# A first attention's scores in 64-row halves, with maxima in single banks

## The reference

```python
scores = jnp.einsum('bhqd,bhkd->bhqk', q, k) / SCALING
att = jax.nn.softmax(scores, axis=-1)
out = jnp.einsum('bhal,bhlv->bhav', att, v)
```

## Time and profile before

| | us |
|---|---|
| median of 3 runs | 1371.28 (1370.59 to 1373.99) |
| profiled execution, its span | 1372.0 |
| TensorE busy in it | 1249.1 |
| VectorE busy | 1009.4 |
| ScalarE busy | 851.8 |
| GpSimd busy | 237.5 |
| line 725, score products, 1024 of them | 312.4 |
| line 612, reductions, 507 of them | 595.8 |
| line 670, exponentials, 1024 of them | 555.6 |

### The profile page before, as it was taken

The page is one execution under the profiler, slowest core; times in us unless marked ns, Lnnn a source line. Parts: engine busy times, 40 slices in busy tenths (PEclk is TensorE's granted clock), DMA queues, the critical chain, the costliest instruction groups (busy, mean ns, idle before and its releaser), DMA issues. The chain is left out here.

```text
span 1372.0 us, 25967 instructions
## 1 busy us (share of the span) xinstructions
PE 1249.1 (91%) x10305; PEld 580.1 (42%) x10305; DVE 1009.4 (74%) x1288; ACT 851.8 (62%) x1447; POOL 237.5 (17%) x309
## 2 busy tenths in 40 slices
PE   6968999999999999999999978998899899899980
PEld 4631222222222222222222225555699566688870
DVE  6878898998899989998999737665676588623324
ACT  3533888888888888888888866555421366533431
POOL 4200110000000000000000002000385222135560
PEclk9986999999999999999999989998999599999995
DMA  5763033232323313222231121100011111123316
GB/s 147 202 199 79 26 65 64 50 76 45 74 64 82 76 40 78 51 66 66 50 74 40 69 71 48 47 16 16 17 31 39 55 44 36 46 69 102 100 58 188
DMA packets 75204, 94.96 MB, mean 69 GB/s; under 512 B 13236, under 2 KB 44684, under 8 KB 74052
## 3 DMA queue, kind: packets, MB, share of 16 engines
q1 hardware_dynamic: 69996, 83.19, 23.9%
q0 software_dynamic: 5088, 10.12, 2.4%
HBM read 54.30 MB, written 38.56 MB: 68 GB/s over the span
## 5 line engine op out<-in xcount | busy, mean ns | idle before, releaser
L670 ACT ACTIVATE b_exp_ring<-psum 128x512 f32<-128x512 f32 x1024 | 555.6, 600 | 148.8 <-PE psum L725 145.6
L612 DVE TENSOR_REDUCE b_mx<-psum 128x2 f32<-128x1024 f32 x507 | 595.8, 1218 | 66.5 <-PE psum L557 65.4
L725 PE MATMUL psum<-b_q,b_k 75*128 75x512 bf16 x1024 | 312.4, 387 | 1.5 <-ACT b_exp_ring L670 1.5
L701 PE MATMUL psum<-b_exp_ring,b_v 128*32 128x512 f32 x2048 | 274.5, 608 | 0.9 <-ACT b_exp_ring L670 0.7
L725 PEld LDWEIGHTS psum<-b_q,b_k 75*128 75x128 bf16 x1024 | 79.3, 97 | 317.0 <-ACT b_exp_ring L670 221.8
L556 PE MATMUL psum<-b_k,b_q 64*128 64x512 bf16 x512 | 168.9, 395 | 25.5 <-DVE b_mx L612 10.6
L557 PE MATMUL psum<-b_ko,b_qo 64*128 64x512 bf16 x512 | 168.9, 395 | 0.0
L740 POOL CAST b_neg<-b_neg_rest 16x128 bf16<-16x128 f32 x32 | 8.9, 279 | 639.6 <-DVE b_neg_rest L623 639.6
L1834 ACT ACTIVATE e_hT<-psum,e_b 128x358 f32<-128x358 f32 (+3 forms) x96 | 53.6, 559 | 75.4 <-PE psum L1854 72.0
L556 PEld LDWEIGHTS psum<-b_k,b_q 64*128 64x128 bf16 x512 | 44.7, 93 | 128.6 <-DVE b_mx L612 41.4
L701 PEld LDWEIGHTS psum<-b_exp_ring,b_v 128*32 128x32 f32 x2048 | 41.3, 108 | 108.6 <-issue 106.0
(11 more groups left out here) (278 smaller groups left out, 1427.6 us busy)
## 6 DMA issues: line engine op xcount, KB each, us to landing
b_q<-q_ops SPq DMA_DIRECT2D x48, 192.0 KB
b_k<-k_ops SPq DMA_DIRECT2D x48, 192.0 KB
k_ops<-a_k SPq DMA_DIRECT2D x20, 256.0 KB, 3.3
x_disp<-b_zeros SPq DMA_DIRECT2D x13, 320.0 KB
e_x<-x_disp SPq DMA_DIRECT2D x8, 520.0 KB
v_ops<-a_vs SPq DMA_DIRECT2D x4, 1024.0 KB, 5.1
b_v<-v_ops SPq DMA_DIRECT2D x16, 256.0 KB
av_out<-b_acc SPq DMA_DIRECT2D x128, 32.0 KB, 1.7
```

The costliest lines, as they stand in the source:

```text
L612: nc.vector.reduce_max(mx[:, d % 2, :, i // 2, i % 2], pair, AX.X).then_inc(sem("b_max_done"), 1)
L670: act.activation(ex[:, n % E_RING, :], g.bank(5 + n % 3), ACT.Exp, scale=ATT_SCALE)\
L701: last = nc.tensor.matmul(AV[32 * i:32 * i + 32, :], v[s][:, at_v:at_v + 32], ex[:, (4 * group + i) % E_RING, :], start=(kb == 0), stop=(k ...
L725: nc.tensor.matmul(g.bank(5 + n % 3), k[s][0:XROWS, h, kb * P:(kb + 1) * P], q[s][0:XROWS, h, half * BANK:(half + 1) * BANK], start=True, ...
```

## The change

The score of 75 rows becomes two products that accumulate in one bank: a main one over 64 rows (q0, k0) and a rest over 64 rows of new tiles (qr, kr), which hold the 8 rows that remain, the three rows of maxima, and zeros against ones. Even heads lie in rows 0 to 63, odd heads in rows 64 to 127, in both the scores and the maxima. q0 and k0 become 128 rows by two heads; qo and ko go. load_quad issues 17 transfers. Each maxima product has one bank of its own (three in turn) and one reduction over 512 columns. Bank 3 takes the values and banks 4 to 7 the scores. On TensorE's queue the four maxima products of a set stand between the products of the scores, and the values come at the end of the group. ScalarE negates the transposed maxima out of their bank, and POOL makes all parts; six transfers instead of three carry them. The maxima now lead by LEAD = 12 groups, FIRST is 10 single products, M_RING is 3 and LOADS0 is 16 * (4 * NPART + 5).

```diff
@@ -197,10 +193,10 @@
     nc, sem = g.nc, g.sem
     g.tiles0 = ExitStack()
     keep = lambda name, shape, dt=F32: g.tiles0.enter_context(nc.sbuf_tensor(name, shape, dt))
-    g.q0 = [keep(f"b_q{c}", [KROWS, HQ, T], BF16) for c in range(SLOTS)]
-    g.k0 = [keep(f"b_k{c}", [KROWS, HQ, T], BF16) for c in range(SLOTS)]
-    g.qo = [keep(f"b_qo{c}", [P, HQ // 2, T], BF16) for c in range(SLOTS)]
-    g.ko = [keep(f"b_ko{c}", [P, HQ // 2, T], BF16) for c in range(SLOTS)]
+    g.q0 = [keep(f"b_q{c}", [P, HQ // 2, T], BF16) for c in range(SLOTS)]
+    g.k0 = [keep(f"b_k{c}", [P, HQ // 2, T], BF16) for c in range(SLOTS)]
+    g.qr = [keep(f"b_qr{c}", [P, HQ // 2, T], BF16) for c in range(SLOTS)]
...
@@ -270,8 +266,8 @@
 
             def first_maximum(n):
                 dve.wait_ge(sem("b_max_scores"), n + 1)
-                pair = g.bank(2 * (n % 2), 2).rearrange("p (h x) -> p h x", h=2)
-                nc.vector.reduce_max(g.mx[:, 0, :, n // 2, n % 2], pair, AX.X).then_inc(sem("b_max_done"), 1)
+                nc.vector.reduce_max(maximum_of(g.mx, n // 4, n % 4), g.bank(n % M_RING), AX.X)\
+                  .then_inc(sem("b_max_done"), 1)
 
             nc.vector.memset(xnT[:, 0:1], 0.0).then_inc(sem("a_const"), 1)
...
@@ -355,9 +352,9 @@
                 if b == 1:
                     pool.wait_ge(sem("a_r28"), 2)
                     for c in range(SLOTS):
-                        nc.gpsimd.memset(g.k0[c][64:KROWS, :, :].rearrange("p h t -> p (h t)").bitcast(F32),
-                                         1.0 + 0x3F80 / 2 ** 23).then_inc(sem("b_ones"), 1)
-                        pool.wait_ge(sem("b_ones"), c + 1)
+                        for rows, word in ((g.kr[c], 1.0 + 0x3F80 / 2 ** 23), (g.qr[c], 0.0)):
+                            nc.gpsimd.memset(rows[:, :, :].rearrange("p h t -> p (h t)").bitcast(F32), word)\
+                              .then_inc(sem("b_ones"), 1)
 
         @block.scalar
...
@@ -426,9 +423,9 @@
             def first_maxima(lo, hi):
 
                 for n in range(lo, hi):
-                    if n >= 2:
-                        pe.wait_ge(sem("b_max_done"), n - 1)
-                    maxima_scores(g, g.q0[0], g.k0[0], g.qo[0], g.ko[0], n, 0, n).then_inc(sem("b_max_scores"), 1)
+                    if n >= M_RING:
+                        pe.wait_ge(sem("b_max_done"), n - M_RING + 1)
+                    maxima_scores(g, 0, n // 4, n % 4, n).then_inc(sem("b_max_scores"), 1)
 
             pe.wait_ge(sem("ident_set"), 1)
...
+        for odd in range(2):
+            rows, heads = slice(MROWS * odd + lo, MROWS * odd + lo + n * HD), slice(odd, HQ, 2)
+            moved(g.q0[c][rows, :, :], g.q_ops[quad, heads, 0:n, :, :].rearrange(flat))
+            moved(g.k0[c][rows, :, :], g.k_ops[quad, heads, m:m + n, :, :].rearrange(flat))
+            if n < NPART:
+                rows = slice(MROWS * odd, MROWS * odd + HD)
+                moved(g.qr[c][rows, :, :], g.q_ops[quad, heads, n:NPART, :, :].rearrange(flat))
+                moved(g.kr[c][rows, :, :], g.k_ops[quad, heads, m + n:m + NPART, :, :].rearrange(flat))
...
+FIRST = 10
+SETS = DUOS * TB
+
+
+def head_rows(odd):
+
+    return slice(MROWS * odd, MROWS * odd + MROWS)
+
+
+def maxima_scores(g, c, x, j, n):
+
+    rows, p, t = head_rows(1 - j // 2), x // TB % 2, x % TB
+    return g.nc.tensor.matmul(g.bank(n % M_RING), g.q0[c][rows, p, t * P:(t + 1) * P],
+                              g.k0[c][rows, p, j % 2 * BANK:(j % 2 + 1) * BANK], start=True, stop=True)
+
+
+def maximum_of(mx, x, j):
...
+    for x in range(SETS + 1):
+        if x < SETS:
+            seq += [(x, j) for j in range(4)]
+        if x and x % TB == 0:
+            seq.append((x // TB - 1, None))
...
+    AV = g.bank(M_RING)
+    SB = M_RING + 1
     seq = max_items()
-    through = lambda kb: 2 * (kb + 1) + (kb >= T_GROUP)
-    upto = lambda d, kb: min(len(seq), ITEMS * (d + 1) - 1 + LEAD + through(kb))
+    place = {item: n for n, item in enumerate(seq)}
+    turned_in = lambda group: (group + LEAD) // TB - 1 if (group + LEAD) % TB == 0 else None
...
+            def maxima(x, which=range(4)):
+                for j in which:
+                    n = place[x, j]
+                    dve.wait_ge(sem("b_max_scores"), n + 1)
+                    nc.vector.reduce_max(maximum_of(mx, x, j), g.bank(n % M_RING), AX.X).then_inc(sem("b_max_done"), 1)
+                d = x // TB
+                if x % TB == TB - 1:
+                    dve.wait_ge(sem("b_max_done"), 4 * (x + 1))
+                    nc.vector.reduce_max(m[:, d % 2, :], mx[:, d % 2, :, :, :].rearrange("p h t a -> p (h t) a"),
+                                         AX.X).then_inc(sem("b_m"), 1)
+
+            maxima(FIRST // 4, range(FIRST % 4, 4))
+            for x in range(FIRST // 4 + 1, LEAD):
+                maxima(x)
...
+            def negated(d):
+                act.wait_ge(sem("b_max_scores"), place[d, None] + 1)
+                if d:
+                    act.wait_ge(sem("b_third"), d)
+                act.activation(neg_all[:, :], g.bank(place[d, None] % M_RING)[0:MAXES, 0:P], ACT.Copy, scale=-1.0)\
+                   .then_inc(sem("b_neg_all"), 1)
+
+            negated(0)
             for d in range(DUOS):
                 for u in range(4 * TB):
                     n = 4 * TB * d + u
+                    if u % 4 == 0 and n and turned_in(n // 4 - 1) is not None and turned_in(n // 4 - 1) < DUOS:
+                        negated(turned_in(n // 4 - 1))
...
+            def turned(d):
+                n = place[d, None]
+                pe.wait_ge(sem("b_m"), d + 1)
+                until_free(pe, n)
+                nc.tensor.transpose(g.bank(n % M_RING)[0:MAXES, 0:P], m[:, d % 2, :], g.ident[:, :])\
+                  .then_inc(sem("b_max_scores"), 1)
+
+            def main_scores(group, i):
+
+                d, kb = group // TB, group % TB
+                s, p, rows, n = d // 2 % SLOTS, d % 2, head_rows(i % 2), 4 * group + i
+                if n >= 4:
+                    pe.wait_ge(sem("b_exp_done"), n - 3)
+                nc.tensor.matmul(g.bank(SB + i), k[s][rows, p, kb * P:(kb + 1) * P],
+                                 q[s][rows, p, i // 2 * BANK:(i // 2 + 1) * BANK], start=True, stop=False)
+
+            def rest_scores(group, i):
+
+                d, kb = group // TB, group % TB
+                s, p, rows = d // 2 % SLOTS, d % 2, head_rows(i % 2)
+                if kb == 0 and i == 0:
+                    pe.wait_ge(sem("b_m_loaded"), 16 * 2 * NPART * (d + 1))
+                nc.tensor.matmul(g.bank(SB + i), kr[s][rows, p, kb * P:(kb + 1) * P],
+                                 qr[s][rows, p, i // 2 * BANK:(i // 2 + 1) * BANK], start=False, stop=True)\
+                  .then_inc(sem("b_scores"), 1)
...
+                main_scores(group, 0)
+                if more:
+                    maxima(x, 0)
+                rest_scores(group, 0)
+                if more:
+                    maxima(x, 1)
+                main_scores(group, 1)
+                main_scores(group, 2)
+                rest_scores(group, 1)
+                rest_scores(group, 2)
+                main_scores(group, 3)
+                if more:
+                    maxima(x, 2)
+                rest_scores(group, 3)
+                if more:
+                    maxima(x, 3)
+                if group:
+                    times_v(group - 1)
+                if turned_in(group) is not None and turned_in(group) < DUOS:
+                    turned(turned_in(group))
...
-                pool.wait_ge(sem("b_max_done"), seq.index((d, None)) + 1)
+                pool.wait_ge(sem("b_neg_all"), d + 1)
+                if d:
+                    pool.wait_ge(sem("b_m_loaded"), 16 * 2 * NPART * d)
+                nc.gpsimd.tensor_copy(neg[:, 0, :], neg_all[:, :]).then_inc(sem("b_first"), 1)
+                pool.wait_ge(sem("b_first"), d + 1)
+                nc.gpsimd.tensor_tensor(neg_rest[:, :], neg_all[:, :], neg[:, 0, :], ALU.subtract)\
+                      .then_inc(sem("b_rest"), 1)
+                pool.wait_ge(sem("b_rest"), d + 1)
...
+                    sp.wait_ge(sem(("b_first", "b_second", "b_third")[i]), d + 1)
+                    for odd in range(2):
+                        row = MROWS * odd + HD + i
+                        dst = qr[d // 2 % SLOTS][row:row + 1, d % 2, :]
+                        sp.dma_start(dst.rearrange("r (t x) -> r t x", x=P), neg[TB * odd:TB * (odd + 1), i, :])\
+                          .then_inc(sem("b_m_loaded"), 16)
```

More of the change, by code:

```diff
@@ L168 @@
 MAXES = 2 * TB
[L169 to L172, removed]
+M_RING = 3
+LEAD = 12
 EARLY = 1
@@ L314, in _ @@
                 if b == B - 1:
-                    first_maximum(0)
+                    for n in range(2):
+                        first_maximum(n)
                 dve.wait_ge(sem("a_sigr"), b + 1)
@@ L321, in _ @@
                 if b == B - 1:
-                    for n in range(1, FIRST):
```

(54 more changed lines are left out.)

80 lines of the change are left out of this document (26 added, 54 removed).

## The result

The changed kernel takes 1328.44 us (median of 4 runs, 1327.96 to 1329.4) against 1370.93 (4 runs, 1368.39 to 1373.99): ratio 0.969, 95% interval 0.9674 to 0.9706, so 42.5 us faster. The forecast was 1336.5, the range 1322 to 1368. The profiled execution took 1328.34 us and spans 1326.6; that of before took 1373.99, the longest of its four, and spans 1372.0. So a run's time and its span are not one figure: the time is some 2 us more in both.

What follows compares the result with a forecast made beforehand. TensorE and its loop with VectorE were taken as the bound. Period 8 x 2.49 + 0.25 + 0.31 = 20.48 against 21.63, times 30.3 is -34.9 us; +0.15 outside the loop gives 1336.5 us, range 1322 to 1368.

Steps and rivals of the forecast that it cites:

- The overlap of halves: TensorE, scores and maxima: one half of the array goes on while the other works, 12 products in six steps of 0.22.
- The rival of seven steps: TensorE: no overlap beyond the pair as written, 2.64 a group, 1373 us, no change; 8% together with reductions 0.66 apart.
- that of bare weight loads: TensorE: steps of 0.31 with weight loads left bare, 2.87 a group, about 1428 us; 6% for this or worse.
- The loop over three banks: Maxima banks: first product, its reduction, last product, values set a group of 2.49 us.
- The fourth score bank: Score banks: four instead of three only loosen ScalarE's side.
- TensorE's own time: TensorE alone needs 2.42 us a group against 2.61.
- Reductions 0.60 apart: VectorE: 512-wide reductions start 0.60 apart, so four cost 2.40 us a group against 2.26.
- The rival at 0.69: VectorE takes over: reductions start as far apart as they last, 2.74 a group, 1390 us; 8%.
- Once per head pair: Small column reduction on VectorE (0.25 stays) and transposition on TensorE (0.31), added to each period's eight groups.
- the rival of late rows: Rows of maxima arrive after the 8.0 us allowed: 1350 to 1368 us; 12% together with waits between halves.
- The start of the stage: Two groups at the low clock lose two changes of shape and a little more, -0.5 us.
- Before the first score: Input stage's ten reductions instead of five, +0.35 us, and the lead's 38 instead of 19, net +0.8.

Runs made afterwards that it cites:

- the ninth kernel: Changed kernel with the heads of the maxima swapped, so each maxima product uses the same half of the array as the score beside it: 1373.96 us.
- The first three experiments: Changed kernel with maxima reductions cut to 256 of 512 columns: only the first of four, 1297.5 us; only the third, 1320.0 us; all four, 1290.8 us.
- the sixth: Changed kernel with two banks for the maxima instead of three, score banks left in place: 1472.56 us.
- seventh experiment: Changed kernel with three score banks and four for the maxima, instead of four and three: 1408.54 us.
- third experiment: Changed kernel with all four maxima reductions of each group reading 256 of 512 columns (wrong output): 1290.8 us.
- the second experiment: Changed kernel with only the third of each group's four maxima reductions reading 256 of 512 columns (wrong output): 1320.0 us.
- the tenth: Changed kernel with the heads of the maxima swapped and all four reductions over 256 columns (wrong output): 1310.34 us.
- the fourth experiment: Kernel before with each maxima reduction reading 256 of the 512 columns in either bank (wrong output): 1359.18 us.

## Why the forecast held, step by step

**The overlap of halves** was the largest unknown, and right: six steps of 0.218 with products of either kind beside each other. The Trainium skill ("TensorEngine Tiling (Array Packing)", Key Properties) says that tiles work independently; the ninth kernel, whose fifth product starts 0.02 us after the first, agrees more strongly than the forecast assumed. The rival of seven steps falls, since a group without the loop takes 2.395 and not 2.64. So does that of bare weight loads: the free steps are 0.21 to 0.23.

**The loop over three banks** was right in mechanism and size: 2.49 forecast, 2.495 measured (a pair is six groups of 2.495, one of 2.60 and one of 2.71). The first three experiments show that it is this loop, and the sixth gives the price of one bank. The fourth score bank, which was to loosen ScalarE's side only, is needed (seventh experiment); the kernel has it, so the forecast didn't suffer.

**TensorE's own time** was forecast at 2.42, measured 2.395 (third experiment). It decided nothing, since the loop lies above it.

**Reductions 0.60 apart** held: the 1014 take up 628.2 us, 0.62 each, though one lasts 0.68. The rival at 0.69 falls. The 0.66 us estimated from the Trainium skill's formula ("VectorE: DVE Perf Modes", TRN2 errata) is near how long one lasts, but they start 0.60 apart, and that counts where they follow each other. (That section's words on small tiles are about operands in SBUF; the formula is its row for reads out of PSUM.)

**Once per head pair** was the term with the wrong size: 0.56 forecast, 0.32 measured (20.28 - 8 x 2.495); 0.24 x 30.3 makes the forecast 7 us too slow. Both of its parts were read from the earlier trace rows as if a gap were a cost. VectorE of the kernel after:

```profile
392.59 1.88 DVE L633 TENSOR_REDUCE b_mx<-psum 128x1 f32<-128x512 f32 x3
394.50 0.19 DVE L637 TENSOR_REDUCE b_m<-b_mx 128x16 f32<-128x32 f32 x1
394.60 2.47 DVE L633 TENSOR_REDUCE b_mx<-psum 128x1 f32<-128x512 f32 x4
```

The next reduction starts 0.10 after the small one. The 0.22 of the earlier trace rows was a wait for a product, the small reduction only hid in it. It costs 0.11, which the second experiment shows by itself. The transposition, and what hangs on it:

```profile
396.65 0.28 PE L714 MATMUL psum<-ident,b_m 128*16 128x128 f32 x1
...
396.86 0.39 PE L723 MATMUL psum<-b_q,b_k 64*128 64x512 bf16 x1
...
396.96 0.27 ACT L683 ACTIVATE b_neg_all<-psum 16x128 f32<-16x128 f32 x1 [0.22 <-PE psum L714]
...
397.61 4.05 SPq L860 DMA_DIRECT2D b_qr<-b_neg  x6
```

It pushes the next product by 0.21, not 0.31: in the earlier trace rows the product behind it had a bank to wait for. The copy takes 0.27 on ScalarE, below both bounds used. The rows of maxima are issued by 401.66, 5.0 us after the transposition, where the forecast had 3.0: it let the issues hide behind POOL's steps, but the six follow one another on SP's queue for 4.05. With a landing of 1.7 that makes 6.7 instead of the forecast's 4.7, with one of 3.6 it would be 8.6, later than the 8.0 at which the rows are wanted. By these numbers the slack of 1.4 wasn't there. TensorE doesn't wait for them in the kernel after, so the rival of late rows falls, but more narrowly than the sum said: with all reductions short it waits once, 0.79 us.

**What the forecast left out.** VectorE had some slack before and has hardly any now, so its rare steps cost more: four pairs that last 0.39 or 0.72 over the others before last 0.71 or 1.03 over after, 1.3 us in all. It takes back a little of the -1.36 x 29 = -39.4.

**The start of the stage** was mis-sized. I gave the low clock -0.5. The stretch to pair 1's values has a mean granted clock of 0.79 before and 0.90 after; with the two levels 0.5 and 1.0, it is 12.0 us at the low one before (0.42 x 28.57) and 4.9 after (0.20 x 24.23). A group of before took 4.77 at the low clock and 2.61 at the full one, so each of these microseconds costs 0.45, and 7.1 fewer give back an estimated 3.2; the rest of the 4.34 is the shorter group. In the kernel after TensorE runs its first values at full speed (123.66). So do the variants of the changed kernel except the tenth. Why the clock rises sooner was not tested. That it's because TensorE idles less ahead of the first score (before, it idles 0.52 us in each 1.13 there) is only a conjecture. For it: the fourth experiment, the old order with gaps of 0.2 to 0.3 there, has a mean clock of 0.82 over 27.71 us (10.0 us at the low level). Against it: in the third one TensorE idled 0.79 us until 112.25 and yet ran its first values at full speed at 116.42.

**Before the first score** +2.40 against +1.15: about 1.0 of it is there before 25 us, where nothing is changed, and varies among the other runs too.

So 1336.5 was 8 us too slow: 7 for the pair's two small steps, about 3 for the clock, less 1.3 for the rare steps and 1.2 for the start.

## What to carry to other kernels

Where a ring of banks ties two engines, walk the loop from the first product through its reduction to the product that reuses the bank; where that loop is the longest, only what lies inside it sets the period (here a shorter reduction inside it gave 0.90 us per head pair, the same beside it 0.11). Before a gap behind a small step is charged to it, look at what ended the gap. When products of 64 rows are put side by side, order them so that the product on which the other engine waits is first in its own half.

No faster version that computes everything was found. Seven banks stand beside the one for values: four for the scores and three for the maxima leave the loop over VectorE (2.50), three and four the one over ScalarE (2.82). That four for each would reach TensorE's 2.395 is only worked out, since there is no ninth bank.

## What the runs showed of the hardware

I had not expected that a product written fifth starts ahead of the second. In the ninth kernel the halves of the array go through their products independently: 0.02 us after the first for the one written fifth, 0.23 for the one written second (again at 401.00 and 401.22 in the group before). And the price of a small VectorE instruction between long ones is 0.10 us, though it is shown as lasting 0.19: a start to the next start is what has to be read, at all sizes (0.10, 0.60 and, for 1024 columns, 1.13).
